# Moving the expert weight folds from the first four steps of an attention and mixture-of-experts kernel to the last three

## The chip, the cores and the metric

One Trainium2 chip, one of its NeuronCores. The metric is the device time of one execution in microseconds (us). A trace of one profiled execution gives every instruction's start and length on TensorE (PE, with its weight loads PEld), VectorE (DVE), ScalarE (ACT), GpSimd (POOL) and SyncE (SP, which issues most transfers).

## The reference

Sixteen images of 128 channels by 256 pixels, float32. A group norm, a linear attention over the pixels with a residual, then per image 256 tokens of 128 features: layer norm, softmax attention with 8 heads of 16, residual, layer norm, and a mixture of 8 experts of which the router takes the best 2 for each token.

```python
x = x + conv_ref(_gn(x), Wq, bq, Wk, bk, Wv, bv, gamma)
t = to_tokens(x)
t = t + attn(ln(t), Wq, Wk, Wv, Wo)
# experts, for the tokens xf = ln(t), gates = the two largest softmax(xf @ router_w + router_b)
h = einsum('td,edh->teh', xf, w1) + b1
gated = silu(einsum('teh,ehf->tef', h, wg) + bg) * (einsum('teh,ehf->tef', h, wv) + bv)
y = einsum('tef,efd->ted', gated, w2) + b2
t = t + einsum('ted,te->td', y, gates)
```

No nonlinearity stands between `w1` and `wg`, `wv`. So the kernel multiplies the weights once, A[e] = w1[e] · [wg[e] | wv[e]] (128 by 512), and the bias is b1[e] · [wg | wv] + [bg | bv].

## The kernel before

**Steps.** The first part is a software pipeline over steps t = 0 to 22. In step t, image t is in the linear attention, image t-1 makes queries, keys and values (split in three bfloat16 parts, sent through DRAM and loaded back stacked), image t-3 computes the row maxima of its scores (banks `MX[0]`, `MX[1]`, 8 passes of `maxima`), image t-4 the scores again and their exponentials (`exps`, banks `EX[0]`, `EX[1]`) and half of the weighting with the values (`weigh`, bank `PV`), image t-5 the other half and the output projection, image t-6 the second layer norm and the router, and image t-7 its tokens' rank in their experts and the scatter of its rows to slots in DRAM. Each engine runs a `step` function of its own, an order written out by hand, with semaphores between them. TensorE executes strictly in that order. The maxima of image t-4 go by a small transfer (`mrow` to `qst`, line 420) into rows 96 to 98 of the stacked queries, and rows 96 to 98 of the stacked keys are ones, so that a score matmul subtracts the maximum; the whole stretch of 32 rows from 96 is set to 1.0 by GpSimd at the start (line 517).

**Folds.** Each of the steps 0 to 3 computes two experts' A (`fold`, line 1163): two halves per expert, each a float32 matmul of 128x128 weights with 128x512, into `EX`, copied out by ScalarE (line 706). `fold_bias` (line 1177) does 8 small matmuls per expert, in two passes each, into `PV`. VectorE copies them out (`brow`, lines 946 and 1025), and at the end of step 3 eight transposes (line 1342) turn them into columns, to which bg and bv are added. Step 4 waits for this. The expert weights (three transfers, 640 KB an expert) are loaded by SyncE at the start between the images, into five buffers, four of which lie in `prob`, the exponentials' tile.

**The stretch between.** When the last image's rows are in their slots, VectorE makes a table of tiles, and 39 tiles of 256 rows go through the experts: SyncE loads a tile's rows when all scatters have landed, TensorE multiplies with `Ae` (a copy of the expert's A), and so on. At step 4 SyncE also issues `b2s` (512 KB), `w2s` (1 MB) and a DRAM to DRAM copy of the spare slots (910 KB, line 454), all behind step 4's own transfers.

## Time and profile before

| | us |
|---|---|
| median of 3 runs | 445.7 |
| lowest and highest | 445.69 and 445.85 |
| the profiled execution | 448.31 |
| its span, first to last instruction | 445.8 |
| TensorE, VectorE, ScalarE, GpSimd busy | 365.0, 299.5, 261.3, 226.3 |

A row of the timeline is: start, length, engine, line, operation, output<-inputs, shape, count, and in brackets the idle time before it with what ended it. A row of the chain is: start, length, engine and line of what the end of the program waited for at that time. Lines are those of the kernel above. A queue row (SPq) is the issue of a transfer, not the transfer.

### The profile page before, as it was taken

Reading aid. Unit: us, or ns where it says so; the run is one execution under the profiler, and the core shown is the slowest. Engines: PE = TensorE matmul, PEld = TensorE weight load, DVE = VectorE, ACT = ScalarE, POOL = GpSimd, SP = SyncE. Lnnn points to the kernel's source line nnn. Section 1 sums busy time; section 2 is a strip of 40 time slices with the busy share of each in tenths; the row PEclk is TensorE's granted clock in tenths of the full one; section 3 lists DMA queues with packets and bytes.
Section 4 is the critical chain, followed back from the end, with each engine's and each line's share of the span. In section 5 each row is a group of like instructions: output and inputs, shape, how many; then the busy total and the mean of one; then the engine's idle time right before and its main releaser. Section 6 shows DMA issues by size and latency. Waiting matters only on the chain.

```text
span 445.8 us, 9570 instructions
## 1 busy us (share of the span) xinstructions
PE 365.0 (82%) x2688; PEld 267.7 (60%) x2688; DVE 299.5 (67%) x1075; ACT 261.3 (59%) x662; POOL 226.3 (51%) x317
## 2 busy tenths in 40 slices
PE   1887878699888898988888785207999999999876
PEld 1353555466556665656555443105988888888776
DVE  5255567589999999999998955532455555555313
ACT  2254447588888888888875652103655566555404
POOL 5122213236666766666675654420667666666710
PEclk9999999899999999999998965557999999999969
DMA  8927428443433444332443000044233333321169
GB/s 248 308 84 203 109 77 288 108 109 88 124 90 99 132 133 119 99 98 85 133 132 97 26 27 24 25 140 122 63 82 93 96 97 89 93 75 48 51 227 350
DMA packets 43219, 52.28 MB, mean 117 GB/s; under 512 B 8208, under 2 KB 35760, under 8 KB 43024
## 3 DMA queue, kind: packets, MB, share of 16 engines
q1 hardware_dynamic: 38208, 40.97, 32.3%
q0 software_dynamic: 4544, 9.38, 6.4%
q10 hardware_dynamic: 416, 1.33, 1.0%
q8 instruction: 22, 0.36, 0.4%
q14 instruction: 29, 0.24, 0.2%
HBM read 33.70 MB, written 19.76 MB: 120 GB/s over the span
## 4 chain that ended last, share of the span: by engine, by line
DVE 30%; PE 22%; ACT 17%; issue 14%; DMA 6%; POOL 4%; SPq 3%; DVEq 2%; ACTq 1%; POOLq 0%
DVE gT L1087 6%; DVE mneg L905 5%; ACT rest L748 4%; PE PV L1153 3%; DVE yb L1095 3%; ACT ys L757 3%; ACT xT L741 2%; PE MX L1131 2%; DMA prob<-res 2%; PE W L1247 2%; PE W L1311 2%; DVE st L912 2%; ACT parts L656 2%; PE EX L1163 1%; PE W L1263 1%
## 5 line engine op out<-in xcount | busy, mean ns | idle before, releaser
L905 DVE TENSOR_REDUCE mneg<-MX 128x2 f32<-128x512 f32 x128 | 84.4, 678 | 7.0 <-PE MX L1131 6.4
L602 ACT ACTIVATE prob<-EX 128x512 f32<-128x512 f32 x128 | 70.9, 598 | 17.7 <-PE EX L1141 16.4
L527 POOL DMA_INDIRECT slots<-rows,dest x64 | 63.3, 989 | 20.3 <-issue 15.6
L1141 PE MATMUL EX<-qst,kst 99*128 99x256 bf16 x256 | 48.5, 287 | 8.4 <-ACT prob L602 4.9
L1131 PE MATMUL MX<-kst,qst 96*128 96x256 bf16 x256 | 49.3, 276 | 3.1 <-DVE mneg L905 3.1
L1384 PE MATMUL W<-w2s,gT 128*128 x312 | 42.7, 280 | 3.4 <-DVE yb L1095 1.8
L1384 PEld LDWEIGHTS W<-w2s,gT 128*128 128x128 f32 x312 | 38.6, 191 | 10.0 <-issue 8.6
L588 POOL DMA_INDIRECT res<-ys,xt x36 | 34.9, 969 | 17.5 <-ACT ys L757 12.0
L1374 PE MATMUL EX<-xT,Ae 128*128 128x256 f32 x156 | 41.0, 387 | 0.0
L1079 DVE COPY Ae<-A 128x512 f32 x39 | 16.6, 429 | 32.6 <-PE PV L1374 19.7
L1141 PEld LDWEIGHTS EX<-qst,kst 99*128 99x128 bf16 x256 | 21.9, 101 | 26.5 <-ACT prob L602 17.6
L1153 PE MATMUL PV<-prob,vaug 128*32 128x256 f32 x512 | 36.0, 401 | 0.9 <-ACT prob L602 0.7
L538 POOL TENSOR_TENSOR onrm<-oT,rden 128x512 f32<-128x512 f32 x16 | 16.7, 1047 | 38.6 <-DVE rden L956 36.2
L547 POOL TENSOR_TENSOR parts<-rest,parts 128x512 bf16<-128x512 f32 x16 | 18.6, 1164 | 32.4 <-ACT parts L674 32.2
L748 ACT ACTIVATE rest<-EX,bias 128x256 f32<-128x256 f32 x78 | 32.6, 471 | 0.0
L1131 PEld LDWEIGHTS MX<-kst,qst 96*128 96x128 bf16 x256 | 23.3, 102 | 12.5 <-issue 5.6
L588 POOL DMA_INDIRECT res<-ys,kvT x16 | 15.5, 970 | 26.6 <-ACT ys L757 24.2
L578 POOL TENSOR_TENSOR rs<-ve,neg_half 128x2 f32<-128x2 f32 x32 | 22.6, 707 | 11.6 <-DVE ve L919 11.1
L1374 PEld LDWEIGHTS EX<-xT,Ae 128*128 128x128 f32 x156 | 27.2, 194 | 2.1
L1087 DVE SCALAR_TENSOR_TENSOR gT<-PV,bias,rest 128x256 f32<-128x256 f32 x40 | 17.5, 480 | 16.0 <-ACT rest L748 13.8
L741 ACT COPY xT<-MX 128x256 f32<-128x256 f32 x39 | 13.7, 352 | 23.4 <-PE MX L1362 18.5
L1087 DVE SCALAR_TENSOR_TENSOR gT<-W,bias,rest 128x256 f32<-128x256 f32 x38 | 16.6, 480 | 14.1 <-ACT rest L748 11.8
(190 smaller groups left out, 838.7 us busy)
## 6 DMA issues: line engine op xcount, KB each, us to landing
qk_parts<-parts SPq DMA_DIRECT2D x16, 384.0 KB, 2.8
qst<-qk_parts SPq DMA_DIRECT2D x16, 192.0 KB
kst<-qk_parts SPq DMA_DIRECT2D x16, 192.0 KB
xt<-slots SPq DMA_DIRECT2D x18, 130.0 KB, 2.1
qst<-qk_parts SPq DMA_DIRECT2D x16, 128.0 KB
kst<-qk_parts SPq DMA_DIRECT2D x16, 128.0 KB
X<-res SPq DMA_DIRECT2D x4, 512.0 KB, 6.7
prob<-res SPq DMA_DIRECT2D x4, 512.0 KB, 7.4
```

The lines of the kernel that those rows point to most:

```text
L527: pool.indirect_dma_start(out=slots, out_offset=bass.IndirectOffsetOnAxis(ap=dest[q][:, n, k:k + 1], axis=0), in_=rows[q][:, n, k, :], in_ ...
L588: pool.indirect_dma_start(out=res, out_offset=bass.IndirectOffsetOnAxis(ap=target[j % LANES][:, k, :], axis=0), in_=ys[j % 4][:, k, :], in ...
L602: act.activation(prob[:, h, :, :], EX[h % 2][:], ACT.Exp, scale=SCALE).then_inc(s["ex_ok"], 1)
L741: act.copy(xT[q][:], MX[q][:, 0, :]).then_inc(s["xT_ok"], 1)
L748: act.activation(sg[q][:, k, :], gate_b[q][:, k, :], ACT.Silu, bias=bias[:, bass.ds(e, 1), k:k + 1].rearrange("p o n -> p (o n)")).then_in ...
L905: dve.tensor_reduce(mneg[p][:, 2 * pair:2 * pair + 2, k], MX[c % 2][:], AX.X, ALU.max, negate=True).then_inc(s["mx_ok"], 1)
L1087: dve.scalar_tensor_tensor(gT[q][:, k, :], val_b[q][:, k, :], bias[:, bass.ds(e, 1), 2 + k:3 + k].rearrange("p o n -> p (o n)"), sg[q][:, ...
L1131: mm = pe.matmul(MX[c % 2][:, u, :], stack(qst, b, h, k * P, P), stack(kst, b, h), start=True, stop=True)
L1141: mm = pe.matmul(EX[h % 2][:, k, :], stack(kst, b, h, k * P, P, QROWS), stack(qst, b, h, rows=QROWS), start=True, stop=True)
L1153: mm = pe.matmul(PV[32 * j:32 * j + 32, g, :], vaug[q][:, k, 4 * g + j, :], prob[:, 4 * g + j, k, :], start=(k == 0), stop=(k == TPB - 1))
L1374: mm = pe.matmul(o, Ae[q][:, f], xT[q][:], start=True, stop=True)
L1384: mm = pe.matmul(y_b[q][:, u, :], gT[q][:, k, u * P:(u + 1) * P], w2s[:, bass.ds(e, 1), k, :].rearrange("p o c -> p (o c)"), start=(k == 0 ...
```

## The change

The folds leave steps 0 to 3. In step 19 (B + 3) TensorE computes experts 0 to 3 into the `MX` banks, which no longer hold scores; in step 20 all eight bias rows into the `EX` banks, their transposes, and experts 4 and 5; at the head of step 21 experts 6 and 7. ScalarE's copies and VectorE's copies move with them. All eight experts' weights are held on chip until then, in tiles of the later part and in images of `X` that have been used; SyncE issues one expert a step at the end of steps 5 to 10, 13 and 16, `b2s` and the slot copy in step 11 and `w2s` in step 14. The three rows of ones come by a transfer in place of the memset. New waits ahead of the tile loop only ask that the folds are done. The diff, cut to its core:

```diff
@@ -45,7 +45,7 @@
-FOLD_BUFS = 5
+EXPERT_AT = (5, 6, 7, 8, 9, 10, 13, 16)
...
@@ -320,20 +312,24 @@
+        xt_more = sb("xt_more", [P, LANES - 6, 2, ROW])
+              + [xt_more[:, p] for p in range(LANES - 6)])
+        Ae_both = sb("Ae_both", [P, 2, 2 * FF])
+        Ae = [Ae_both[:, p, :] for p in range(2)]
+        gT_both = sb("gT_both", [P, 2, FF // P, PAIR])
+        gT = [gT_both[:, p] for p in range(2)]
-        spare_w = prob[:].rearrange("p (i g) k n -> p i (g k n)", i=FOLD_BUFS - 1)
-        fold_w = [wgv[:]] + [spare_w[:, i, :].rearrange("p (k n) -> p k n", k=FF // P) for i in range(FOLD_BUFS - 1)]
-        fold_1 = [w1s[:]] + [t[:] for t in ys]
-        brow = [t[:].rearrange("p a r -> p (a r)") for t in oT]
+        fold_w = [wgv[:], Ae_both[:], gT_both[:].rearrange("p q k n -> p q (k n)"),
+                  xt_more[:].rearrange("p l k c -> p (l k c)")[:, 0:4 * FF].rearrange("p (k n) -> p k n", k=FF // P)]
+        fold_w += [X[:, 4 * i:4 * i + 4, :].rearrange("p (k h) n -> p k (h n)", k=FF // P) for i in range(E - 4)]
+        fold_1 = [w1s[:]] + [v[:] for v in ys] + [v[:] for v in yb] + [xT[0][:].rearrange("p (k c) -> p k c", c=C)]
+        brow = [v[:] for v in rest]
...
@@ -388,26 +384,19 @@
-                i = e % FOLD_BUFS
-                need(sp, s["fbias_mm"], e - FOLD_BUFS + 1)
-                sp.dma_start(fold_1[i], w1_t[e].rearrange("(k f) d -> f k d", f=P)).then_inc(s[f"fold_ld{e}"], 16)
+                if e >= 4:
+                    sp.wait_ge(s["xn_ok"], 4 * (e - 3))
+                    sp.wait_ge(s["xs_ok"], 4 * (e - 3))
+                sp.dma_start(fold_1[e], w1_t[e].rearrange("(k f) d -> f k d", f=P)).then_inc(s[f"fold_ld{e}"], 16)
-                    sp.dma_start(fold_w[i][:, :, n * FF:(n + 1) * FF], w[e].rearrange("(k f) n -> f k n", f=P)
+                    sp.dma_start(fold_w[e][:, :, n * FF:(n + 1) * FF], w[e].rearrange("(k f) n -> f k n", f=P)
-            load_images(0)
-            load_expert(0)
-            load_images(1)
-            sp.dma_start(b1c[:], b1.rearrange("e f k -> f e k")).then_inc(s["bgv_ld"], 16)
-            for n, v in enumerate((bg, bv2)):
-                sp.dma_start(bgvr[2 * E * n:2 * E * (n + 1), :], v.rearrange("e (k f) -> (e k) f", f=P)
-                             ).then_inc(s["bgv_ld"], 16)
-            load_expert(1)
-            load_images(2)
-            load_expert(2)
-            load_expert(3)
-            load_images(3)
-            load_expert(4)
+            for g in range(len(GN)):
+                load_images(g)
+            sp.dma_start(kst[STACK:QROWS, :, :].rearrange("p r n -> p (r n)").bitcast(F32),
+                         pad[PADS].rearrange("p c -> (p c)")[0:(QROWS - STACK) * RING * H * N // 2].rearrange(
+                             "(p n) -> p n", p=QROWS - STACK)).then_inc(s["one_ld"], 16)
@@ -442,18 +431,21 @@
-                if t == 0:
-                    load_expert(5)
-                if t == 1:
-                    load_expert(6)
-                    load_expert(7)
+                for e, at in enumerate(EXPERT_AT):
+                    if t == at:
+                        load_expert(e)
                 if t == RAMP:
+                    sp.dma_start(b1c[:], b1.rearrange("e f k -> f e k")).then_inc(s["bgv_ld"], 16)
+                    for n, v in enumerate((bg, bv2)):
+                        sp.dma_start(bgvr[2 * E * n:2 * E * (n + 1), :], v.rearrange("e (k f) -> (e k) f", f=P)
+                                     ).then_inc(s["bgv_ld"], 16)
+                if t == RAMP + 7:
                     sp.dma_start(b2s[:], b2.partition_broadcast(P)).then_inc(s["b2_ld"], 16)
+                    sp.dma_start(slots[E * SLOTS:, :].rearrange("(a r) c -> a (r c)", a=P),
+                                 pad[E:PADS].rearrange("t p c -> (t p) c").rearrange("(a r) c -> a (r c)", a=P)
+                                 ).then_inc(s["pad_st"], 16)
+                if t == RAMP + 10:
                     sp.dma_start(w2s[:], w2.rearrange("e (k f) c -> f e k c", f=P)).then_inc(s["w_ld"], 16)
-                    sp.dma_start(slots[E * SLOTS:, :].rearrange("(a r) c -> a (r c)", a=P),
-                                 pad[E:].rearrange("t p c -> (t p) c").rearrange("(a r) c -> a (r c)", a=P)
-                                 ).then_inc(s["pad_st"], 16)
...
@@ -514,10 +508,8 @@
             pool.wait_ge(s["g_rstd"], 1)
-            pool.memset(kst[STACK:P, :, :], 1.0).then_inc(s["z_pool"], 1)
-            pool.wait_ge(s["z_pool"], 6)
             pool.memset(ones[:], 1.0).then_inc(s["ones_ok"], 1)
-            met = (s["z_pool"], 6)
+            met = (s["z_pool"], 5)
@@ -623,9 +615,16 @@
+            def folded(*experts):
+                for e in experts:
+                    act.wait_ge(s["fold_mm"], e + 1)
+                    act.copy(pick(A, e), MX[e % 2][:].rearrange("p a n -> p (a n)")).then_inc(s["A_ok"], 1)
             def step(t, p):
                 e = live(t - 4)
+                if t == B + 5:
+                    folded(4, 5, 6)
                 if live(t - 1):
@@ -679,6 +678,8 @@
                              ).then_inc(s["vaug_ok"], 1)
+                if t == B + 3:
+                    folded(0, 1)
                 b, q = t - 1, o
@@ -700,10 +701,6 @@
                     head_exp(t - 4, 4)
-                for n in folds(t):
-                    act.wait_ge(s["fold_mm"], n + 1)
-                    act.copy(pick(A, n), EX[n % 2][:].rearrange("p a n -> p (a n)")).then_inc(s["A_ok"], 1)
                 if e:
@@ -719,6 +716,10 @@
                     act.copy(mrow[q][:], W[2][0:3 * H * TPB, 0:P // 2].bitcast(BF16)).then_inc(s["mT_ok"], 1)
+                if t == B + 3:
+                    folded(2, 3)
+                if t == B + 5:
+                    folded(7)
...
@@ -919,6 +922,12 @@
+            def bias_rows(i):
+                dve.wait_ge(s["lo_ok"], B)
+                dve.wait_ge(s["fbias_mm"], 4 * i + 4)
+                dve.tensor_copy(brow[i], EX[i][:].rearrange("p a n -> p (a n)")).then_inc(s["brow_ok"], 1)
             def step(t, p):
@@ -941,9 +950,6 @@
                     group_variance(*GN[t + 1], t + 1)
-                if t == 2:
-                    dve.wait_ge(s["fbias_mm"], 4)
-                    dve.tensor_copy(brow[0], PV[:].rearrange("p a n -> p (a n)")).then_inc(s["brow_ok"], 1)
                 if live(t - 7):
@@ -954,6 +960,12 @@
                     dve.reciprocal(rden[q][:], oT[q][:, :, HD]).then_inc(s["rden_ok"], 1)
+                if t == B + 3:
+                    dve.wait_ge(s["bgvT_mm"], 1)
+                    dve.tensor_copy(bgvT[:], MX[1][:, 0, 0:4 * E]).then_inc(s["bgvT_ok"], 1)
+                    dve.wait_ge(s["bgvT_ok"], 1)
+                if t == B + 4:
+                    bias_rows(0)
                 row_maxima(1, 2)
@@ -1016,13 +1028,8 @@
                     pass
-                if at_step(t, 0):
...
-                if t == RAMP - 1:
-                    dve.wait_ge(s["fbias_mm"], E)
-                    dve.tensor_copy(brow[1], PV[:].rearrange("p a n -> p (a n)")).then_inc(s["brow_ok"], 1)
+                if t == B + 4:
+                    bias_rows(1)
                     for i in range(2):
...
@@ -1158,26 +1167,41 @@
                     pe.wait_ge(s[f"fold_ld{e}"], 48)
+                    pe.wait_ge(s["mx_ok"], B * H)
                     need(pe, s["A_ok"], e - 1)
-                i = e % FOLD_BUFS
-                mm = pe.matmul(EX[e % 2][:].rearrange("p a n -> p (a n)"), fold_1[i][:, k, :], fold_w[i][:, k, :],
+                    if e == 1:
+                        pe.wait_ge(s["bgvT_ok"], 1)
+                mm = pe.matmul(MX[e % 2][:].rearrange("p a n -> p (a n)"), fold_1[e][:, k, :], fold_w[e][:, k, :],
                                start=(k == 0), stop=(k == FF // P - 1))
-            def fold_bias(e):
...
+            def fold_whole(*experts):
+                for e in experts:
+                    for k in range(FF // P):
+                        fold(e, k)
+            def fold_bias(*experts):
+                for e in experts:
+                    pe.wait_ge(s[f"fold_ld{e}"], 48)
+                    pe.wait_ge(s["ex_ok"], B * H)
+                    i, at = e // 4, e % 4 * P
+                    for k in range(FF // P):
+                        for n in range(4):
+                            mm = pe.matmul(EX[i][32 * n:32 * n + 32].rearrange("p a n -> p (a n)")[:, at:at + P],
+                                           b1c[:, e, k:k + 1].broadcast_to([P, 32]),
+                                           fold_w[e][:, k, n * P:(n + 1) * P],
+                                           start=(k == 0), stop=(k == FF // P - 1))
+                    mm.then_inc(s["fbias_mm"], 1)
+            def bias_to_columns(i):
+                pe.wait_ge(s["brow_ok"], i + 1)
+                for n in range(4):
+                    mm = pe.transpose(EX[i][:].rearrange("p a n -> p (a n)")[:, n * P:(n + 1) * P],
+                                      brow[i][:, n * P:(n + 1) * P], ident)
+                mm.then_inc(s["browT_mm"], 1)
@@ -1206,12 +1230,12 @@
                 if t == RAMP:
-                    pe.wait_ge(s["z_pool"], 6)
+                    pe.wait_ge(s["z_pool"], 5)
+                    pe.wait_ge(s["one_ld"], 16)
                     pe.wait_ge(s["ones_ok"], 1)
                     pe.wait_ge(s["idb_ok"], 2)
-                    pe.wait_ge(s["bias_ok"], 2)
-                for e in folds(t)[:1]:
-                    fold(e, 0)
+                if t == B + 5:
+                    fold_whole(6, 7)
                 b, q = t - 4, p
@@ -1230,6 +1254,8 @@
                     weigh(t - 5, o, 1)
+                if t == B + 4:
+                    fold_bias(0, 1, 2, 3)
                 if t in (1, 2):
@@ -1257,6 +1283,11 @@
                     mm.then_inc(s["t3_mm"], 1)
+                if t == B + 3:
+                    pe.wait_ge(s["bgv_ld"], 48)
+                    pe.wait_ge(s["mx_ok"], B * H)
+                    pe.transpose(MX[1][:, 0, 0:4 * E], bgvr[:], ident[0:4 * E, 0:4 * E]).then_inc(s["bgvT_mm"], 1)
+                    fold_whole(0)
                 b, q = t - 1, o
@@ -1278,6 +1309,10 @@
                     mm.then_inc(s["rt_mm"], 1)
+                if t == B + 3:
+                    fold_whole(1)
+                if t == B + 4:
+                    fold_bias(4, 5, 6, 7)
                 maxima(3)
@@ -1288,8 +1323,6 @@
                 maxima(4)
-                for e in folds(t)[:1]:
-                    fold(e, 1)
                 exps(0)
@@ -1297,8 +1330,6 @@
                     pe.matmul(W[1][:, 0:N], vkz[q][:], qz[q][:], start=True, stop=True).then_inc(s["out_mm"], 1)
-                for e in folds(t)[1:]:
-                    fold(e, 0)
                 exps(1)
@@ -1311,7 +1342,16 @@
                     mm.then_inc(s["wo_mm"], 1)
+                if t == B + 3:
+                    fold_whole(2)
+                if t == B + 4:
+                    bias_to_columns(0)
+                    fold_whole(4)
+                    bias_to_columns(1)
+                    fold_whole(5)
                 exps(2)
+                if t == B + 3:
+                    fold_whole(3)
                 maxima(6)
@@ -1322,27 +1362,10 @@
                 maxima(7)
-                for e in folds(t)[1:]:
-                    fold(e, 1)
-                for e in folds(t):
-                    fold_bias(e)
-                if at_step(t, 0):
-                    pe.wait_ge(s["bgv_ld"], 48)
-                    pe.transpose(MX[1][:, 0, 0:4 * E], bgvr[:], ident[0:4 * E, 0:4 * E]).then_inc(s["bgvT_mm"], 1)
                 exps(4, 5)
                 exps(6, 7)
-                if t == RAMP - 1:
...
             steps(pe, step, B + 7)
...
```

## Rows read from the trace of the kernel before

**Rows 1.** The page, busy us and share of each engine over the span

```profile
PE 365.0 (82%) x2688; PEld 267.7 (60%) x2688; DVE 299.5 (67%) x1075; ACT 261.3 (59%) x662; POOL 226.3 (51%) x317
```

**Rows 2.** Windows by step: stretch, length, busy us (count) PE, PEld, DVE, ACT, POOL, clock, DMA

```profile
0.00:25.70 25.70, 13.68 (x68) 7.25 (x68) 12.97 (x51) 6.59 (x13) 9.15 (x15) 1.00 0.87 260
25.70:37.60 11.90, 9.24 (x68) 5.12 (x68) 6.95 (x35) 5.81 (x13) 3.02 (x4) 1.00 0.37 116
48.40:62.10 13.70, 11.22 (x87) 6.91 (x87) 8.71 (x20) 5.97 (x14) 2.85 (x7) 1.00 0.27 66
62.10:74.00 11.90, 10.66 (x90) 6.37 (x90) 8.05 (x18) 9.43 (x21) 2.87 (x7) 1.00 0.65 170
74.00:91.10 17.10, 13.03 (x98) 8.32 (x98) 10.64 (x28) 9.71 (x22) 4.80 (x10) 0.90 0.55 171
91.10:104.10 13.00, 11.86 (x105) 8.11 (x105) 12.10 (x50) 11.58 (x30) 4.74 (x10) 1.00 0.34 92
257.60:282.40 24.80, 16.76 (x90) 10.20 (x86) 12.68 (x68) 9.46 (x26) 12.89 (x16) 0.52 0.07 23
```

**Rows 3.** Timeline of the first 26 us: the memset, and the kvT addition in step 1

```profile
7.05 5.21 POOL L517 MEMSET kst<- 32x6144 bf16 x1
...
25.52 0.46 DVE L936 TENSOR_TENSOR kvT<-W,cs 128x288 f32<-128x288 f32 x1
```

**Rows 4.** The chain that ended last, steps 0 and 1

```profile
9.38 2.97 DVE kvT L936
...
13.84 1.91 PE EX L1163 x2
15.75 0.97 PE W L1247 x4
...
26.10 0.54 PE W L1247 x4
...
31.47 0.97 POOL grstd L511
```

**Rows 5.** The same chain in step 3

```profile
52.81 0.86 PE EX L1163 x2
...
57.22 1.05 PE PV L1177 x32
58.30 0.70 DVE oT L1025
59.05 1.09 PE EX L1342 x8
```

**Rows 6.** Timeline of steps 4 and 5: slot copy's issue, step 5's first head scores

```profile
69.93 4.49 SPq L454 DMA_DIRECT2D slots<-in_pad  x1
...
81.48 0.61 PE L1141 MATMUL EX<-qst,kst 99*128 99x256 bf16 x2 [3.07 <-DMA qst<-mrow]
```

**Rows 7.** Timeline of a filled step: SyncE's issues, the first head scores

```profile
102.86 1.78 SPq L420 DMA_DIRECT2D qst<-mrow  x3
...
108.58 0.38 PE L1141 MATMUL EX<-qst,kst 99*128 99x256 bf16 x2
...
110.42 0.38 SPq L443 DMA_DIRECT2D qk_parts<-parts  x1
...
115.89 1.78 SPq L420 DMA_DIRECT2D qst<-mrow  x3
```

**Rows 8.** Window of 2 us in step 19

```profile
264.00:266.00 2.00, 2.00 (x16) 0.75 (x19) 1.86 (x15) 1.41 (x3) 1.63 (x2) 0.50 0.21 71
```

**Rows 9.** Timeline of steps 19 to 21: exponentials, projection, rank, router

```profile
267.43 1.08 ACT L602 ACTIVATE prob<-EX 128x512 f32<-128x512 f32 x2 [1.81 <-PE EX L1141]
...
273.50 2.08 PE L1311 MATMUL W<-cs,ao 128*128 128x128 f32 x8 [0.90 <-DVE ao L962]
...
279.18 0.20 PE L1227 MATMUL W<-mask,tri 128*128 128x16 bf16 x1 [3.61 <-DVE cum L876]
...
281.35 1.02 PE L1278 MATMUL W<-cs,x2T 128*128 128x8 f32 x4 [0.46 <-ACT x2T L651]
```

More of the change, by code:

```diff
@@ L121, in live @@
     return not isinstance(b, int) or 0 <= b < B
-def folds(t):
-    return range(2 * t, 2 * t + 2) if t < RAMP else ()
-def at_step(t, at):
-    return isinstance(t, int) and t == at
 def within(j):
@@ L470, in _ @@
             sp.wait_ge(s["ao_ok"], B)
+            sp.wait_ge(s["fold_mm"], E)
+            sp.wait_ge(s["fbias_mm"], E)
             for j in range(ST):
@@ L733, in _ @@
             act.wait_ge(s["lo_ok"], B)
+            act.wait_ge(s["fold_mm"], E)
+            act.wait_ge(s["fbias_mm"], E)
             act.wait_ge(s["bias_ok"], 2)
@@ L1073, in _ @@
             dve.wait_ge(s["b2_ld"], 16)
+            dve.wait_ge(s["fold_mm"], E)
+            dve.wait_ge(s["fbias_mm"], E)
+            dve.wait_ge(s["A_ok"], E)
             for j in range(-2, ST + 1):
@@ L1166, in fold @@
                     mm.then_inc(s["fold_mm"], 1)
-            def fold_bias(e):
-                if e == 0:
-                    pe.wait_ge(s["bgv_ld"], 48)
-                if e == E // 2:
-                    pe.wait_ge(s["brow_ok"], 1)
-                i, at = e % FOLD_BUFS, e % (E // 2) * P
-                for k in range(FF // P):
-                    for n in range(4):
-                        mm = pe.matmul(PV[32 * n:32 * n + 32].rearrange("p a n -> p (a n)")[:, at:at + P],
-                                       b1c[:, e, k:k + 1].broadcast_to([P, 32]), fold_w[i][:, k, n * P:(n + 1) * P],
-                                       start=(k == 0), stop=(k == FF // P - 1))
-                mm.then_inc(s["fbias_mm"], 1)
+            def fold_whole(*experts):
[20 more added lines that the diff above has]
+                mm.then_inc(s["browT_mm"], 1)
             def step(t, p):
@@ L1335, in step @@
                 exps(6, 7)
-                if t == RAMP - 1:
-                    pe.wait_ge(s["brow_ok"], 2)
-                    pe.wait_ge(s["A_ok"], E)
-                    for i in range(2):
-                        for n in range(4):
-                            mm = pe.transpose(EX[i][:].rearrange("p a n -> p (a n)")[:, n * P:(n + 1) * P],
-                                              brow[i][:, n * P:(n + 1) * P], ident)
-                        mm.then_inc(s["browT_mm"], 1)
             steps(pe, step, B + 7)
@@ L1353, in _ @@
             pe.wait_ge(s["w_ld"], 16)
+            pe.wait_ge(s["A_ok"], E)
+            pe.wait_ge(s["bias_ok"], 2)
             words = expert_words(pe, packed)
```

17 lines of the change are left out of this document (5 added, 12 removed).

## The prediction

> **What bounds the kernel now.** I read the page's busy shares first. TensorE 82%, VectorE 67%, ScalarE 59% [rows 1]: no engine is full, so I cut the span at the token transposes that open each step and read the stages [rows 2]. Steps 1 and 4, 11.9 us each, have TensorE busy 9.2 and 10.7 us. Step 3 takes 13.7. Step 5 takes 17.1 where its neighbours take 11.9 and 13.0, at a mean clock of 0.90. From there to 257.6 us VectorE fills the step and nothing of the change touches it. From there to the last router matmul (257.6 to 282.4) TensorE is busy 16.8 of 24.8 us at a clock of 0.52, nearly all at the lower of its two levels, 1.2 GHz. The reader is to see two things: the front holds matmul work that may not set its length, and the end holds idle TensorE time inside a chain of short dependent operations. So the question for each fold is not whether an engine is idle but what stands behind the fold in TensorE's order.
>
> **The start.** The 5.21 us memset of constant rows is removed [rows 3]. The addition behind it took 2.97 us in step 0 and 0.46 in step 1 [rows 3, 4]; both engines come free together at 12.3. Without it the addition ends at 9.85, three statistics and their sums reach TensorE at about 11.8 instead of 13.24: 1.45 us. Then the first fold half goes, 1.91 us, which is the pace of 1.2 GHz against 0.86 later (the clock column shows no change there) [rows 4, 5], and with it another like it, of which the query copy would have hidden most; the output matmul ends at 15.95 by my count instead of 20.15. Term: **-4.2 us**; bounds -3.35 (only memset and first fold) and -5.4 (memset and both). The load that replaces the memset is 36 KB behind the images, wanted four steps later: nothing; uncovered it would cost some 2 us, like the small loads.
>
> **Steps 1 and 2.** Each had four fold halves of 0.86 us and 32 bias matmuls of 1.05 together [rows 5], 4.5 in all, leaving some 4.8 of TensorE's 9.24 us in step 1 [rows 2]. I expect no gain. The chain runs from the scores' copies over GpSimd's subtraction to GpSimd's root (31.47) [rows 4], which VectorE waits for before the next statistics; the folds stood in that gap. Bounds: 0 and -0.7 each.
>
> **Step 3.** Here folds are on the chain: one of 0.86 us ahead of the output matmul, 32 bias matmuls of 1.05, a bank copy of 0.70, and eight transposes of 1.09, after which step 4 begins at 60.1 [rows 5]. Counting the order without them: output 0.86 us earlier, last maximum at 56.0, its parts at 57.3, step 4's normalised tokens at 58.3 instead of 61.2. Term: **-3.0**; bounds -0.9 and -3.7 (the four pieces).
>
> **Step 5.** The queue of SyncE spends 4.49 us issuing the copy of spare slots, with the 512 KB and 1 MB loads before it, and the maxima's rows that step 5's scores need stand behind it. TensorE idles 3.07 us for them [rows 6] and falls to 1.2 GHz: a mean of 0.90 over 17.1 us [rows 2] is 3.4 us at half speed, which costs up to 1.7; I take 1.5. Term: **-4.6**, which brings 17.1 to 12.5, between its neighbours [rows 2]; bounds -3.1 and -5.2. The loads now stand in steps 11 and 14. In a filled step SyncE issues the store at 110.42 and the next rows at 115.89 [rows 7]: 5.1 us are free, the bias load and the slot copy need about 5.3, so the rows go out 0.2 late. Rows issued by 104.64 are wanted at 108.58 [rows 7]: 3.9 us in which to land, so 0.2 is nothing. Expert loads need three issues of half a microsecond in the same gap. I take 0; uncovered, the old stall of 4.6 is the upper bound.
>
> **The clock in the front.** This speaks against the change. Steps 1 to 3 ran at 2.4 GHz with TensorE busy 9.2 of 11.9 us; now it is 4.8, and by my count there are 4 to 5 us of nothing between step 1's last transposes and step 2's means. Step 5 shows that a 3.07 us wait was followed by 1.2 GHz. The same matmul group took 0.97 us at the lower and 0.54 at the upper level [rows 4]; the means, token transpose, this group and the query and key matmuls are 2.3 us of the chain in each step. I take them at the lower level in steps 1 and 2, 1.6 each, and partly in step 3, 1.3. Term: **+4.5**; bounds 0 (stays up, as before) and +7 (all chain matmuls of step 3 too, some 4 us). The Trainium skill (TensorE: Matmul & The Clock Gate, What's actually happening) makes the lower level the default that only activity lifts. Going by that page alone I would take the +7 end; the trace agrees in that it starts at the lower level and fell back after a wait.
>
> **The end.** Added on TensorE, in its order, at 2.4 GHz: 16 fold halves of 0.86 [rows 5], 13.8; 64 pairs of bias matmuls (four times 1.05), 4.2; the transposes, 1.1. That is 19.1 us; the question is what waits. I walked the order from 258.1. Each bank copy costs 0.54 on ScalarE [rows 9] (a like pass) and 0.70 on VectorE.
> Step 19: fold 0 before the router matmul, fold 1 before the first scores, and ScalarE's copies of both before the router's and the heads' exponentials; folds 2 and 3 between scores. The last head exponential ends at 271.1 instead of 268.5.
> Step 20: second weighting 271.25 to 272.3, four bias folds, then token transposes and router matmul to 275.8, four bias folds to 277.8, output projection to 278.8. Before, that projection started at 273.50 and took 2.08 at the lower level; now its add comes 3.2 us later. The router ends at 282.5, VectorE copies the second bias bank only then (283.2), and TensorE, which waits for it after fold 4, goes on to the transposes and fold 5 at 285.5.
> Step 21: folds 6 and 7 stand first: 288.9. Behind them are the rank matmul (before: 279.18), the last token transposes and the last router matmul (before: 281.35, 1.02 us; now 290.4, 0.55) [rows 9]. So the last router starts 8.6 us late and everything behind it, scatter, table, first slot load, moves along.
> These took the upper level. Before, the clock was down for nearly the whole stretch, and 2.00 of 2.00 busy microseconds of head scores and weighting did not lift it [rows 8]; the folds of the start did, and I expect these to, after 1.5 us lost. Term: **+10.1**; bounds +4 (19.1 less the 8.0 us that TensorE idles up to the last router matmul [rows 2], less some 7 that its own matmuls there gain at 2.4 GHz) and +30 (38.2 at 1.2 GHz less the same 8.0).
>
> **Sum.** -4.2 - 3.0 - 4.6 + 4.5 + 10.1 = +2.8. On the profiled execution: span 445.8 to 448.6, its own time 448.31 to 451.1. That execution lies 2.6 above the median of the runs, 445.7; the same difference on the median gives **448.5 us**.
>
> **Rivals.**
> (a) *The front keeps 2.4 GHz* (the other side). Then +4.5 falls away: 444.0. For it: nearly unbroken matmuls from the means to the query, some 5 us a step, and three steps at full clock in [rows 2]. Against: the folds were half of that work. It decides once the clock costs under 1.9 us. Chance 0.20.
> (b) *The front stays at 1.2 GHz through step 3*: +7, 451.0. Chance 0.12. The Trainium skill's page on the clock gate would lead here.
> (c) *The stall only moves* to step 11 or 14: +4.6, 453.1. The slot copy fills SyncE's gap to the last 0.2 us; against: no 1 MB load stands before it now. Chance 0.07.
> (d) *The end runs at 1.2 GHz*: +30 in place of +10.1, 468. For: [rows 8]; against: full-width matmuls without gaps. Chance 0.04.
> (e) *The folds at the end hide better*, half way to their bound, +7: 445.4; with part of (a), 444. For it: VectorE's and GpSimd's own latencies between those matmuls; against: in-order TensorE, with folds 6 and 7 plainly ahead of the last rank. Chance 0.07.
> (f) *The front gives less*: the chain over GpSimd hides fold removal in steps 0 and 3 to the lower bounds, 3.0 less: 451.5. Chance 0.05.
> My forecast: 0.45, its own range 446 to 451.
>
> **How the numbers follow.** About 0.2% (0.9 us) is what a measurement of this kernel can tell from no change. The forecast's 0.45 gives 0.36 slower, 0.06 same, 0.03 faster; (a) 0.17 faster and 0.03 same; (e) 0.04 and 0.03; the others, 0.28, slower. Faster 0.24, same 0.12, slower 0.64. The range 443.5 to 453.5 leaves out (d) and the ends of (a) and of the clock's cost joined to (c).
>
> **What would show it.** Right: the first token transposes near 21.5 instead of 25.7; steps 1 and 2 at 12.5 to 13.5 us, with the group of four at 0.9 us and not 0.54; step 5 near 12.5 with no wait for the maxima's rows; first slot load 2 to 3 us later than 298.3, while the stretch from the last head exponential's step to it has grown by 9 to 11. Wrong: upper clock in the front; a wait of the head scores for their rows in step 11, 12, 14 or 15; the rank matmul of step 21 not behind the folds; folds of over 1.5 us per half at the end.

## The result: slower by 2.2%, the front and one stall undersized

| | kernel before | kernel after |
|---|---|---|
| median | 445.74 us | 457.27 us |
| ratio, 95% interval | 1 | 1.0218 (1.0175 to 1.026) |
| profiled execution, its span | 448.31, 445.8 us | 456.24, 454.3 us |

The forecast was 448.5 (443.5 to 453.5), the likelier side slower. The side was right, the size was not: 8.8 us too low, and outside the range. The interval of the ratio lies clear of 1; whether the loss is above or below 2% it does not settle. The page of the kernel after, busy us and shares, and the clock in 40 slices of 11.4 us, against [rows 1]:

```profile
PE 366.0 (81%) x2688; PEld 266.5 (59%) x2688; DVE 295.5 (65%) x1075; ACT 261.0 (57%) x662; POOL 221.3 (49%) x316
...
PEclk9997669999999999999999998856999999999989
```

TensorE issues the same 2688 matmuls (366.0 us busy against 365.0), VectorE and GpSimd have less to do; TensorE's clock is low in slices 4 to 6, between 34 and 68 us, and again in slices 25 to 28, from 273 us. The windows by step (columns as in [rows 2]):

```profile
0.00:21.60 21.60, 7.92 (x25) 4.94 (x25) 9.49 (x50) 5.62 (x11) 3.93 (x14) 1.00 0.41 136
21.60:35.60 14.00, 6.89 (x28) 3.93 (x28) 7.01 (x34) 4.78 (x11) 3.02 (x4) 0.89 0.28 75
35.60:48.00 12.40, 6.47 (x28) 3.65 (x28) 3.93 (x16) 4.77 (x11) 3.64 (x4) 0.78 0.26 69
48.00:60.90 12.90, 9.37 (x42) 4.97 (x42) 7.38 (x17) 5.04 (x12) 2.85 (x7) 0.76 0.26 68
60.90:74.80 13.90, 13.15 (x90) 7.23 (x90) 8.04 (x18) 9.44 (x21) 2.87 (x7) 0.80 0.38 89
74.80:87.10 12.30, 11.33 (x97) 7.28 (x97) 10.60 (x28) 9.47 (x22) 4.77 (x10) 1.00 0.58 152
165.30:182.40 17.10, 13.57 (x109) 8.71 (x105) 12.79 (x53) 11.66 (x30) 8.70 (x14) 0.90 0.31 91
256.00:306.30 50.30, 30.07 (x262) 17.45 (x258) 23.44 (x117) 14.25 (x37) 19.62 (x22) 0.82 0.14 44
306.30:454.30 148.00, 133.70 (x830) 118.86 (x830) 68.33 (x162) 72.48 (x204) 75.90 (x78) 0.96 0.36 114
```

Cut at the same instructions as the kernel before (marks unrounded, hence hundredths), these and all runs below give this table. One column is one stretch, and a cause should move one column. "End" is from step 19's second-norm transposes to the first slot load, "tiles" from there to the span's end.

```
us                    start  1 to 4  step 5  6 to 11  step 12  13 to 18   end   tiles
before                25.69   48.31   17.08    78.62    13.03     74.90  40.64  147.53
after                 21.58   53.17   12.37    78.16    17.13     73.67  50.22  148.00
predicted change       -4.2    +1.5    -4.6        0        0         0  +10.1       0
measured change        -4.1    +4.9    -4.7     -0.5     +4.1      -1.2   +9.6    +0.5
slotcopy_step4        21.75   53.67   12.37    78.19    13.03     74.53  49.96  148.30
b2s_step4             21.75   52.51   12.36    78.19    13.19     75.06  48.44  146.90
filler_in_front       23.54   46.62   12.37    78.19    20.47     73.60  50.23  148.58
before_late_loads     25.14   48.32   12.38    78.64    17.61     73.72  41.39  148.10
before_ones_load      23.09   48.30   18.09    78.63    13.03     73.45  40.15  147.46
folds_behind_routers  21.76   53.20   12.37    78.19    16.84     75.01  41.30  151.53
all_mended            22.02   47.97   12.37    78.17    13.47     75.00  41.64  153.36
loads_and_ones        23.45   48.33   12.38    78.63    13.03     74.67  37.58  147.93
step0_folds_last      24.96   49.79   12.37    79.82    13.09     75.83  40.04  160.60
after_two_mends       21.83   47.98   12.37    79.03    13.23     74.65  53.04  161.87
after_again           21.85   53.91   12.38    79.68    14.69     75.73  51.68  160.88
w2s_step4             22.59   49.68   13.13    78.64    13.04     74.68  37.56  147.78
```

Two terms that had been set to nothing or too low are the miss: steps 1 to 4 and step 12. In the timeline of the kernel after (start, duration, in brackets the idle time before and who ended it):

```profile
9.27 0.46 DVE L945 TENSOR_TENSOR kvT<-W,cs 128x288 f32<-128x288 f32 x1 [2.04 <-PE W L1225]
...
22.18 1.04 PE L1273 MATMUL W<-kvT 128*16 128x128 f32 x4
...
158.94 0.54 SPq L443 DMA_DIRECT2D b2s<-in_b  x1
159.52 0.75 SPq L444 DMA_DIRECT2D slots<-in_pad  x1
...
159.89 0.96 POOL L519 DMA_INDIRECT slots<-rows,dest  x1 [0.30 <-issue]
...
168.25 0.88 ACT L615 ACTIVATE rows<-T,nb,rs 128x128 f32<-128x128 f32 x2 [3.47 <-DMA slots<-rows,dest]
169.19 0.69 PE L1284 MATMUL W<-cs,rows 128*128 128x128 f32 x2 [2.38 <-ACT rows L615]
...
281.55 5.30 PE L1174 MATMUL MX<-X,yb 128*128 128x512 f32 x8
285.17 0.58 ACT L621 COPY A<-MX 128x512 f32<-128x512 f32 x1 [5.59 <-PE MX L1174]
...
288.40 0.17 PE L1251 MATMUL W<-mask,tri 128*128 128x16 bf16 x1
```

The addition to kvT takes 0.46 us, not 2.97 [rows 3, 4]. The group of four matmuls takes 1.04 us in step 1, the lower clock level; in the same view of the kernel before it takes 1.04 in step 0 and 0.61 in step 1 (0.97 and 0.54 in the chain, whose rows are shorter [rows 4]). The clock went up and down inside the steps: it was 1.00 until 29.3 us, 0.77 in the 5.8 us that followed without a single matmul, 0.59 in the first 5.1 us of step 2, and 1.00 again from 40.2. In step 12 ScalarE waits 3.47 us before it may overwrite `rows`, because scattered rows of step 11 (the buffer's last user, two images back), the last issued at 159.89, have not landed; SyncE had issued the bias broadcast and the slot copy in that same microsecond. At the end the rank matmul of step 21 starts 9.2 us later than before [rows 9], right behind folds 6 and 7.

### The profile page after: what moved, and what is told of

Read it like the earlier page. It is cut to its first block, busy times and chain, and to the rows that moved or that the text cites. A ratio compares the mean times of both kernels' runs of the same rounds, so it can differ in the third digit from the quotient of the medians.

```text
span 454.3 us, 9591 instructions
## 1 busy us (share of the span) xinstructions
PE 366.0 (81%) x2688; PEld 266.5 (59%) x2688; DVE 295.5 (65%) x1075; ACT 261.0 (57%) x662; POOL 221.3 (49%) x316
## 4 chain that ended last, share of the span: by engine, by line
DVE 29%; PE 28%; ACT 16%; issue 11%; DMA 6%; POOL 3%; SPq 2%; DVEq 2%; ACTq 1%; POOLq 0%
DVE mneg L908 6%; DVE gT_both L1097 5%; PE PV L1162 4%; ACT rest L751 3%; PE MX L1174 3%; DVE yb L1105 3%; ACT ys L760 3%; PE W L1273 2%; PE MX L1140 2%; DMA prob<-res 2%; ACT xT L744 2%; PE W L1294 2%; ACT prob L594 2%; PE W L1295 2%; DMA slots<-rows,dest 2%
## 5 line engine op out<-in xcount | busy, mean ns | idle before, releaser
L1150 PE MATMUL EX<-qst,kst 99*128 99x256 bf16 x256 | 45.9, 274 | 6.1 <-ACT prob L594 4.7
L1409 PE MATMUL W<-w2s,gT_both 128*128 x312 | 42.9, 281 | 2.6 <-DVE yb L1105 1.5
L1409 PEld LDWEIGHTS W<-w2s,gT_both 128*128 128x128 f32 x312 | 38.7, 191 | 9.0 <-issue 7.9
L580 POOL DMA_INDIRECT res<-ys,xt_more x36 | 35.2, 978 | 17.0 <-ACT ys L760 11.5
L1399 PE MATMUL EX<-xT,Ae_both 128*128 128x256 f32 x156 | 41.4, 390 | 0.0
L1089 DVE COPY Ae_both<-A 128x512 f32 x39 | 16.7, 430 | 32.9 <-PE PV L1399 19.9
L1162 PE MATMUL PV<-prob,vaug 128*32 128x256 f32 x512 | 34.3, 385 | 1.1 <-ACT prob L594 0.9
L1399 PEld LDWEIGHTS EX<-xT,Ae_both 128*128 128x128 f32 x156 | 27.6, 197 | 2.2
L1097 DVE SCALAR_TENSOR_TENSOR gT_both<-PV,bias,rest 128x256 f32<-128x256 f32 x40 | 17.6, 480 | 15.9 <-ACT rest L751 11.7
L1097 DVE SCALAR_TENSOR_TENSOR gT_both<-W,bias,rest 128x256 f32<-128x256 f32 x38 | 16.6, 479 | 13.3 <-ACT rest L751 11.0
```

The source lines that it names most:

```text
L580: pool.indirect_dma_start(out=res, out_offset=bass.IndirectOffsetOnAxis(ap=target[j % LANES][:, k, :], axis=0), in_=ys[j % 4][:, k, :], in ...
L1097: dve.scalar_tensor_tensor(gT[q][:, k, :], val_b[q][:, k, :], bias[:, bass.ds(e, 1), 2 + k:3 + k].rearrange("p o n -> p (o n)"), sg[q][:, ...
L1150: mm = pe.matmul(EX[h % 2][:, k, :], stack(kst, b, h, k * P, P, QROWS), stack(qst, b, h, rows=QROWS), start=True, stop=True)
L1162: mm = pe.matmul(PV[32 * j:32 * j + 32, g, :], vaug[q][:, k, 4 * g + j, :], prob[:, 4 * g + j, k, :], start=(k == 0), stop=(k == TPB - 1))
L1399: mm = pe.matmul(o, Ae[q][:, f], xT[q][:], start=True, stop=True)
L1409: mm = pe.matmul(y_b[q][:, u, :], gT[q][:, k, u * P:(u + 1) * P], w2s[:, bass.ds(e, 1), k, :].rearrange("p o c -> p (o c)"), start=(k == 0 ...
```

## The experiments

Ratios are to the kernel before in the same comparison. The span of one execution is the coarser measure: executions of the kernel before alone lay between 443.7 and 450.2 us (the last comparison apart, below), so single columns of the table carry more than totals. The 0.2% that the prediction took as the smallest change a measurement can tell was too small for this kernel.

### Step 12: which of the two transfers

One run puts the slot copy back into step 4, the other the bias broadcast.

```diff
+                if t == RAMP:
+                    sp.dma_start(slots[E * SLOTS:, :]...).then_inc(s["pad_st"], 16)
                 if t == RAMP + 7:
                     sp.dma_start(b2s[:], b2.partition_broadcast(P)).then_inc(s["b2_ld"], 16)
-                    sp.dma_start(slots[E * SLOTS:, :]...).then_inc(s["pad_st"], 16)
```

> The kernel after, with the copy of the slot table (pads) alone moved back from SP's step 11 to its step 4; the bias broadcast (b2s) stays in step 11. Theory 1: that copy, two transfers in DRAM, holds back the landing of GpSimd's scattered rows of step 11, on which ScalarE's rows of step 12 wait 3.47 us. Then step 12 (165.28 to 182.41, 17.1 us) is 13.1 again and the kernel near 453, a little more if step 5 takes some of it back (up to +4.7, when the copy goes out late there as before). Rival: the broadcast of b2s does it; then step 12 stays at 17.1 and the time near 457.

> The kernel after, with the bias broadcast (b2s) alone moved back to SP's step 4 and the slot copy left in step 11: the mirror of the run before. Theory 1 (the slot copy holds back the scatters): step 12 stays at 17.1 us, time near 457. Rival (the broadcast does it): step 12 is 13.1, time near 453.

Measured: 452.99 us, ratio 1.0117 (1.0057 to 1.0177), and 452.50 us, 1.0121 (1.0064 to 1.0179). The first run did what its theory said, the second what its rival said, and the two answers contradict each other if one transfer is the cause: step 12 is 13.03 and 13.19 us, the stall is gone in both. So it takes both transfers together (512 and 910 KB), and neither alone is "the cause". With the slot copy alone in step 11, a wait of 0.96 us is left, and TensorE covers it:

```profile
165.27 0.88 ACT L616 ACTIVATE rows<-T,nb,rs 128x128 f32<-128x128 f32 x2 [0.96 <-DMA slots<-rows,dest]
```

ScalarE goes on right after the slot copy has landed. The copy took 8.2 us from its issue at 159.52 in the kernel after, 6.5 us from 158.45 here:

```profile
slots<-in_pad SPq DMA_DIRECT2D x1, 910.0 KB, 8.2
slots<-in_pad SPq DMA_DIRECT2D x1, 910.0 KB, 6.5
```

ScalarE starts 0.5 and 0.3 us after its landing (168.25 and 165.27), and 0.2 to 0.3 us after it in two profiles below (filler_in_front: 9.3 us from 154.96; before_late_loads: 9.1 from 158.50). The Trainium skill (DMA: Bandwidth & Descriptors, Queues, rings and completion order) says why another queue's copy can matter: the write that signals completion lands only after every earlier write of the same DMA engine, whichever queue it came from. These runs agree with it (8.4 us from the last scatter's issue at 159.89 to ScalarE's start, right behind the copy's landing), but do not separate it from plain sharing of bandwidth.

### The front: is it the clock?

```diff
+            def idle(e):
+                if e < 2 * RAMP:
+                    pe.matmul(EX[e % 2][:]..., ident, cs[:, 0:2 * FF], start=True, stop=True)
+            def idle_columns(e):  # the same for the 8 bias matmuls, into PV
...
                 maxima(4)
+                idle(2 * t)
                 exps(0)
```

> The kernel after, with idle matmuls of the kernel before's size and at its places in steps 0 to 3 (16 of 128x128 by 128x512 and 64 of 32 columns), on tables already on chip and into banks that nothing reads: TensorE's load of before in front without its loads, waits and copies. Theory A: what the front lost against the forecast (steps 1, 2 and 4 longer by 2.05, 1.65 and 2.04 us, and step 3 shorter by only 0.9 where 3.0 was expected) is the granted clock; then steps 1 to 4 run at 1.00 granted, come to 10.8 to 12.2 us each, the kernel gains 4 to 8 us (449 to 453) and the runs lie within 1 us of each other. Rival: the longer steps come from something else that left with the folds (the order of DMA queues, the ones load), and the idle matmuls cost their own time: no gain, or up to 4 us more (457 to 461).

Measured: 455.36 us, ratio 1.0139 (1.0067 to 1.021). Theory A holds for the steps: all four at a granted clock of 1.00, together 46.6 us instead of 53.2. The windows of steps 1 to 4, and of step 12 (here busy time of PE alone, then clock, DMA share, GB/s):

```profile
23.50:35.50 12.00, 9.34 (x69) 1.00 0.24 64
35.50:46.20 10.70, 9.17 (x68) 1.00 0.41 107
46.20:58.30 12.10, 10.24 (x79) 1.00 0.28 72
58.30:70.20 11.90, 10.70 (x90) 1.00 0.48 104
...
160.70:181.20 20.50, 16.16 (x110) 0.75 0.26 77
```

More matmul work, and 6.6 us less time: nothing waits for these matmuls, and no load or copy came back with them. The total gained less, and 455.36 missed the 449 to 453 expected, for two reasons outside the four steps. The start is 1.9 us longer, because two of the idle matmuls stand in step 0's chain; and step 12 stalled for 7.4 us this time (20.5 against 13.0), with a mean clock of 0.75 over that step. The runs did not come within 1 us of each other (450.81 to 455.43), so that part of the expectation failed.

### The parts that were meant to gain, put into the kernel before

```diff
-                if t == RAMP:
+                if t == RAMP + 7:
                     sp.dma_start(b2s[:], ...)
+                    sp.dma_start(slots[E * SLOTS:, :]..., pad[E:]...)
+                if t == RAMP + 10:
                     sp.dma_start(w2s[:], ...)
-                    sp.dma_start(slots[E * SLOTS:, :]..., pad[E:]...)
```

> The kernel before, with only the loads moved: b2s and the slot copy from SP's step 4 to step 11, w2s to step 14, as in the kernel after. Step 5 should be 12.4 us instead of 17.1 (-4.7). Theory 1 (the stall of step 12 comes with the place of the slot copy alone): step 12 takes 17.1 instead of 13.1, net near 445.2. Rival (the stall needs what else changed, the expert loads in steps 5 to 13): no stall, near 441.

Measured: 448.20 us, ratio 1.0005 (0.9964 to 1.0046). Theory 1, by the columns: step 5 is 12.38 us, step 12 is 17.61, with the same wait, in a kernel that has neither expert loads there nor folds at the end:

```profile
167.91 0.88 ACT L623 ACTIVATE rows<-T,nb,rs 128x128 f32<-128x128 f32 x2 [4.14 <-DMA slots<-rows,dest]
```

So the gain of step 5 and the stall of step 12 cancel. The constant rows alone (memset of kst out, the 36 KB load in, behind the last expert load of the front):

> The kernel before, with only the constant rows changed: the load in the place of GpSimd's memset of kst. The theory of the start: the memset costs the front about 1.5 us through VectorE's copy to kvT behind it (the rest of the -4.1 of the start being the two folds of step 0 and their copies), so the first token transposes stand at 24.2 instead of 25.7 and the kernel gains about 1.5 us. Rival: the memset is the larger part of the start, 3 us or more; or the copy is then held by the next thing and nothing comes.

Measured: 446.43 us, ratio 0.9952 (0.9924 to 0.998). The start is 23.09 us: 2.6 less than in the first profile of the kernel before, 2.1 less than in the run above, which has that kernel's start. Not all of that is the memset. The matmul on the second group's sums, which waits for VectorE, stands 8.31 and 8.32 us behind the first group's in the two kernels with the memset and 6.7 behind it here and in the later runs without it: the memset itself is worth 1.6 us, close to the 1.45 of the prediction. The rest is the clock. The second half of fold 0, two matmul passes behind the first chain matmuls, took 2.08 us in the kernel before, the lower level throughout, 1.55 in before_late_loads, which still has the memset, and 1.40 here. In two later runs with the folds in front and no memset it took 1.65 and 1.12, and their starts are 23.45 and 22.59:

```profile
11.58 0.59 PE L1112 MATMUL MX<-gagg,cs 128*128 128x6 f32 x2 [2.35 <-DVE gagg L791]
...
15.83 1.65 PE L1166 MATMUL EX<-wgv,w1s 128*128 128x512 f32 x2
```

```profile
11.61 0.59 PE L1111 MATMUL MX<-gagg,cs 128*128 128x6 f32 x2 [2.35 <-DVE gagg L790]
...
15.47 1.12 PE L1165 MATMUL EX<-wgv,w1s 128*128 128x512 f32 x2
```

So the same start lies up to 0.9 us apart by the moment at which the clock rises, and the two folds of step 0 were worth 1.0 to 2.4 us of it; the idle matmuls put 1.96 back (21.58 to 23.54). In this run step 5 took 1.0 us more than in the kernel before (18.09, mean clock 0.81 against 0.90), which eats part of the gain.

### The end: TensorE's order or the router's chain?

```diff
+                if t == B + 5:
+                    fold_whole(0, 1)
+                if t == B + 6:
+                    fold_whole(2, 3)
...
             pe.matmul(W[0][:, 0:E], ones[:], cend[:], ...).then_inc(s["cnt_mm"], 1)
+            fold_bias(0, 1, 2, 3)
+            fold_bias(4, 5, 6, 7)
+            fold_whole(4)
+            bias_to_columns(0)
+            fold_whole(5)
+            bias_to_columns(1)
+            fold_whole(6, 7)
```

> The kernel after, with the folds placed otherwise: two experts ahead of each of the last two waits for the ranks of VectorE's router (3.6 and 4.4 us of idle TensorE each), and the bias products, the other four folds and the transposes behind the counting matmul, where TensorE is idle for 12.2 us; the copies out of the banks by ScalarE. Theory C: the end's +9.6 us lies in TensorE's own order in the steps that follow step 19 (16.2 and 16.7 us there against 12.8 and 9.8 before). Then these are 13 and 10 again, the slot loads start 7 to 10 us earlier, and the first tile starts 0 to 4 us later behind them: 448 to 452, and the first tiles at 2.4 GHz may give up to 1 us more. Rival: what is late in the end is the router's chain on VectorE and ScalarE, for which it does not matter where the folds stand: no gain.

Measured: 452.48 us, ratio 1.0075 (1.0033 to 1.0117). Just above the range expected. Theory C holds: the end falls from 50.2 to 41.3 us, 0.7 above the kernel before, with all of the bias rows and all but about one and a half of the eight experts' folds done by then. The tiles took 3.5 us more than after's 148.0:

```profile
301.37 0.59 ACT L622 COPY A<-MX 128x512 f32<-128x512 f32 x1 [1.13 <-PE MX L1164]
```

```profile
305.69 1.11 PE L1370 MATMUL MX<-cs,kvT 128*128 128x128 f32 x4 [4.37 <-issue]
```

The first is ScalarE's copy of the last fold, the second TensorE's first tile transposes: 7.0 us behind the first slot load (298.67) instead of 2.1. TensorE's last fold matmul ends at 301.3, and only then does it read its table of experts, 4.4 us in which no wait shows. In the kernel after that reading was over while TensorE waited for the first slots.

### Together

> The kernel after with the three repairs: the slot copy in step 4, the folds behind the last routers, and idle matmuls in steps 0 to 3 (none ahead of the step's transposes in step 0, so that the start keeps its -4.1). If the three losses are separate, they add: -4 (step 12), -8 (end), -6 (front, -4.6 measured with the start's loss of 1.9 included), from 455 to some 437 to 441, 5 to 9 us below the kernel before. If they share a cause or a cover, less: 443 to 447.

Measured: 444.44 us, ratio 0.9900 (0.9846 to 0.9955). Against the kernel after the columns add nearly as they did singly: steps 1 to 4 -5.2, step 12 -3.7, end -8.6; the tiles give +5.4 back. The median is above the 437 to 441 expected by about those 5 us. Of the four steps one fell short: step 2 took 12.10 us at a mean clock of 0.86, where filler_in_front took 10.76 at 1.00. Two kernels with the real folds in front show the same (w2s_step4 12.10, step0_folds_last 12.22, both 0.86), so neither folds nor idle matmuls hold the clock every time. The idle matmuls buy the clock, but pay nothing else. So the next run is the opposite combination: folds left in front, where they are useful filler, and only the loads and the rows of ones changed (the slot copy in step 4).

> The kernel before, with only the parts of the change that gained: the load of the constant rows, b2s in step 11 and w2s in step 14, and the slot copy left in step 4; the folds stay in front. Separate gains: -1.5 (start) and -4.7 (step 5), no stall in step 12: 439.5 to 441.5. Rival: the slot copy in step 4 keeps part of step 5's stall, 443 to 445.

Measured: **439.98 us against 448.34, ratio 0.9821 (0.9784 to 0.9858)**, the lowest ratio of the study. Start -2.2, step 5 -4.7, step 12 unchanged:

```profile
66.05 0.59 SPq L455 DMA_DIRECT2D slots<-in_pad  x1
...
70.98 2.49 SPq L424 DMA_DIRECT2D qst<-mrow  x3
```

That is 6.9; the end of this profile is also 3.1 us shorter (37.58), its step 19 with the clock at 1.00 (0.54 in the kernel before). So the median hit the expected range partly by luck: about a third of the gain is none of the expected terms. The next run shows the same end (37.56, clock 1.00). Why the clock was up there in these two and not in the kernel before was not tested.

One more run asks which of the three loads had held step 5.

```diff
                 if t == RAMP:
                     sp.dma_start(slots[E * SLOTS:, :]..., pad[E:PADS]...)
+                    sp.dma_start(w2s[:], ...)
```

> The kernel before with the load of the constant rows and b2s in step 11 (as in the best run so far), but w2s back in step 4 and behind the slot copy there, where the kernel before has it ahead of it. Theory: what held step 5 is the load of w2s (1 MB), whose transfers fill the queue, so that whatever is issued behind it waits: here the maxima's rows themselves; then step 5 takes 16 to 18 us again and the kernel is near 0.992 of the one before. Rival: it was the order, the slot copy's issue behind w2s (4.49 us there, 0.59 when it goes alone); then step 5 takes 12.4 and the ratio stays near 0.982.

Measured: 439.99 us, ratio 0.9863 (0.9785 to 0.994). Mostly the rival: step 5 takes 13.13 us, not 17. The 1 MB load in front of the rows costs 0.8 us; putting the slot copy ahead of that load and b2s out of the step saves 4:

```profile
66.54 0.59 SPq L455 DMA_DIRECT2D slots<-in_pad  x1
67.59 0.86 SPq L458 DMA_DIRECT2D w2s<-in_w  x1
71.46 1.84 SPq L424 DMA_DIRECT2D qst<-mrow  x3
```

The same copy was 4.49 us in issue behind w2s [rows 6] and is 0.59 ahead of it. (This run also has b2s out of step 4, which stood ahead of w2s there, so the order and b2s are not separated. Behind b2s alone the slot copy took 0.75 us, line 444 above, and b2s alone in step 4 left step 5 at 12.36.)

### Three runs beside a slower kernel before

In this comparison the kernel before itself took 462.41 us, its successors in proportion; the front's columns are near those elsewhere, the tiles are 13 us longer. Only ratios and columns are used.

> The kernel of the run before (the kernel before with the ones load, b2s in step 11, w2s in step 14), with the two folds of step 0 put at the end of TensorE's step 0 instead of among its chain. If what is left of the start's difference (23.4 us to the first token transposes there, 21.6 in the kernel after) is TensorE's waiting for and computing these folds ahead of the chain, the first transposes stand at 22 and the kernel is 1 to 1.5 us under 440. Rival: ScalarE's copies of the two folds then hold step 1's normalization, step 1 grows by as much, no gain.

```diff
+                if t == 0:
+                    for e in folds(0):
+                        fold(e, 0)
+                        fold(e, 1)
```

Measured: ratio 0.9889 (0.9848 to 0.993). The rival, and stronger: the start is 24.96 us, 1.5 more than in loads_and_ones. ScalarE's second bank copy stands ahead of step 1's normalization and waits for fold 1:

```profile
22.29 0.58 ACT L709 COPY A<-EX 128x512 f32<-128x512 f32 x1 [1.30 <-PE EX L1166]
22.77 0.88 ACT L626 ACTIVATE tn<-T,nb,rs 128x128 f32<-128x128 f32 x2
```

> The kernel after with the slot copy in step 4 and the idle matmuls in steps 0 to 3 (none in the chain of step 0), the folds left in the last steps. The difference to the kernel after is then the front's clock plus the stall of step 12: -4.6 to -6 and -4.1, so about 9 to 10 us below it, 446 to 448, and the runs lie closer together than the kernel's own. Rival: the two are not additive (one is hidden by the other): 450 or more.

> The kernel after unchanged, beside the others on the same chip: about 1.02 times the kernel before, 455 to 458, and runs up to 5 us apart. Step 12 long and the front at the same places as in its first profile if these are properties of the kernel and not of that one execution.

Measured: ratios 1.0088 (1.0051 to 1.0124) and 1.0258 (1.0202 to 1.0315); medians 466.50 and 473.63, a difference of 7.1 us, less than the 9 to 10 expected. The front is 6.0 us shorter (75.8 to 69.8 at the start of step 5), as expected. The stall of step 12 was only 1.3 to 1.7 us in the unchanged kernel here, not 4.1:

```profile
169.61 0.88 ACT L615 ACTIVATE rows<-T,nb,rs 128x128 f32<-128x128 f32 x2 [2.28 <-DMA slots<-rows,dest]
```

So the front's loss is a property of the kernel (53.2 and 53.9 us); the size of the step 12 stall is not: it was 1.3 to 7.4 us in the four profiles of the kernel after and its variants that have both transfers in step 11, and 4.6 in the kernel before with them there.

## Why the prediction was wrong in size, step by step

- **The start, -4.2: -4.1.** Right, in the mechanism too: the memset gave 1.6 (1.45 forecast), the folds 2.4 (2.75 forecast), and 0.1 came from the first image, which landed earlier. That the folds gave so much hung on one profile of the kernel before, in which the clock rose late; against the others they would have given 1.0 to 1.9.
- **Steps 1 to 4, clock +4.5 and step 3 -3.0: +4.9 for +1.5. This step failed.** The mechanism was the one named, but both of its terms were mis-sized. The prediction put the lower level on 2.3 us of matmuls in the chain of each step, for steps 1, 2 and part of 3. In fact step 4 too began at the lower level (granted 0.50 from 60.9 to 65.0 us, 1.00 from 67.0) and took 2.0 more, a step that had no term, and step 3 gave 0.9 instead of 3.0 less 1.3, since its larger share of matmuls ran slow as well. The experiment with idle matmuls separates the two terms: without the folds' waits and copies but with the clock at 1.00 the four steps take 46.6 us, 1.7 less than before, all of it in step 3 (-3.0 forecast; the idle matmuls still take their own time there); and the clock's price on top is 6.6 us, against 4.5 forecast and a bound of 7. Rival (b), to which 0.12 was given, is nearest. The Trainium skill's page that was quoted for it (TensorE: Matmul & The Clock Gate, HAM oscillation) also says what helps, there against waits for DMA: order the work so that TensorE has no long gaps. The runs agree: filler made four steps 6.6 us shorter.
- **Step 5, -4.6: -4.7.** Right, and the cause is now narrower: the 1 MB load alone costs 0.8 us; most of the stall came with the slot copy behind b2s and w2s in SyncE's queue. It needs w2s there (behind b2s alone the copy was issued in 0.75 us); whether w2s alone is enough was not run.
- **Steps 11 and 14, 0: +4.1 in step 12.** This failed too. The prediction looked for what SyncE would issue late, and that part held: the maxima's rows were in time. It did not look at whose transfers share the DMA engines: GpSimd's scatters, on which ScalarE waits two images later, in none of the rows read. Rival (c) has the size but another mechanism. Whether the scatters waited for the copy's writes or only shared the DMA engines with them stays open.
- **The end, +10.1: +9.6.** Right, in the mechanism too: moving the folds behind the routers took 8.9 of it away. The clock was at 1.00 from 256 to 280 us, so rival (d) falls. The last tenths are luck: the 1.5 us set aside for the clock were not lost at the start of step 19. They were lost after TensorE's wait for VectorE's copy in step 20: from there to the rank matmul the mean clock was 0.80, and the eight matmul passes of folds 5 and 6 took 5.30 us (281.55 above), where the four of fold 7 took 1.88. In b2s_step4, at 1.00 from 255 to 285 us, the end is 48.4, 7.8 more than before, close to rival (e)'s +7.
- **What was left out.** The other steps were 1.7 us shorter; 1.2 of that is steps 13 to 18, which vary as much (73.5 to 75.1) between kernels in which they are the same. By spans the forecast was +2.8 and +8.5 came: 5.7 too low, 3.4 from the front, 4.1 from step 12, less 1.7 from these, the rest small. The remaining 3.1 of the 8.8 are in the reference: the profiled execution of before lay 2.6 us above its median, that of after 1.0 below, less 0.6 between time and span. The forecast carried the 2.6 over to the kernel after, which no row supported.

## What to carry to other kernels

Work that an idle stretch of TensorE already hides may be holding its clock for the chain around it: before it is moved away, price the whole stretch at the lower level until the engine is dense again, and not only the matmuls on the chain. A bulk transfer that is moved must be held against every transfer that is in flight at its new place, on all queues, and against its neighbours in its own: behind a 512 KB and a 1 MB load the same copy took its queue 4.49 us, ahead of the 1 MB load 0.59. And when a set of edits loses, try the parts alone: the loads' part of this change, with one transfer put elsewhere, was 1.8% faster than the kernel before, some two thirds of it by the expected terms.

## What the runs showed that had not been expected

- Leaving matmuls out made steps longer: steps 1 to 4 took 53.2 us without the folds (granted clock 0.76 to 0.89) and 46.6 with idle matmuls at their places (1.00).
- Two transfers (512 and 910 KB) issued 0.6 us apart by SyncE held a scatter of GpSimd's queue for up to 9.2 us from its issue (8.4 in the kernel after, 155.32 to 164.51 in filler_in_front); either of them alone left a wait of at most 1.2 us (all_mended), and steps of 13.0 to 13.5.
- One 5.21 us memset on GpSimd cost the front 1.6 us: VectorE's cast beside it took 5.25 us and takes 0.23 without it, and its addition 2.97 and 0.46.
- Neither the real folds nor idle matmuls held the clock every time: step 2 took 10.76 us at 1.00 or 12.1 to 12.2 at 0.86, in kernels with either.
- The same kernels were 3% slower in one comparison, most of it in the tiles (160.9 us against 148.0 in the kernel after, 12.9 of 16.5 us) while the front kept its times to about a microsecond. What differed there is not known.
